# Scores of the fourth attention as three float32r passes over split queries and keys

## The reference

```
k = einsum('ihd,bpd->biph', W_K, x)          # 16 heads of 128, all from 256 inputs
q = einsum('ihd,bpd->biph', W_Q, x)
v = einsum('ihd,bpd->biph', W_V, x)
scores = einsum('biph,biqh->biqp', k, q)     # causal mask, then divided by sqrt(128)
attn = softmax(masked / sqrt(d_head))
z = einsum('biqp,biph->biqh', attn, v)
out = einsum('df,bqf->bqd', W_O, z_flat)
```

## Time and profile before

| | before |
|---|---|
| median of 3 runs (lowest, highest) | 1263.75 us (1261.93, 1264.17) |
| the profiled execution | 1260.36 us |
| its span in the profile | 1258.3 us |
| mean granted clock of PE | 0.986 |
| busy: PE, DVE, ACT, POOL | 93%, 57%, 47%, 14% |

### The profile page before, as it was taken

The page is one execution under the profiler, slowest core; times in us unless marked ns, Lnnn a source line. Parts: engine busy times, 40 slices in busy tenths (PEclk is TensorE's granted clock), DMA queues, the critical chain, the costliest instruction groups (busy, mean ns, idle before and its releaser), DMA issues.

```text
span 1258.3 us, 18298 instructions
## 1 busy us (share of the span) xinstructions
PE 1165.3 (93%) x6204; PEld 773.3 (61%) x6204; DVE 722.7 (57%) x2031; ACT 594.2 (47%) x1498; POOL 175.5 (14%) x225
## 2 busy tenths in 40 slices
PE   5889988898999978999999989989999999999999
PEld 4644444523267554665656558877777777776877
DVE  3778726847144278878797870164444444446573
ACT  2635553677822223554545550255555555555140
POOL 3240023421500400000000010120111121210000
PEclk8979999999999989999999999999999999999999
DMA  8001100140222600000000000220000000000001
GB/s 240 25 8 42 48 30 1 46 141 1 101 70 78 234 0 18 13 13 14 9 9 9 9 1 1 92 96 10 21 22 18 17 26 18 18 9 2 1 1 34
DMA packets 26894, 48.65 MB, mean 39 GB/s; under 512 B 3774, under 2 KB 20126, under 8 KB 25734
## 3 DMA queue, kind: packets, MB, share of 16 engines
q1 hardware_dynamic: 24070, 38.13, 9.5%
q0 software_dynamic: 2736, 9.37, 2.5%
HBM read 40.36 MB, written 9.19 MB: 39 GB/s over the span
## 4 chain that ended last, share of the span: by engine, by line
PE 73%; DVE 13%; ACT 6%; issue 4%; POOL 2%; DMA 1%; SPq 0%; ACTq 0%; DVEq 0%; POOLq 0%
PE bank L1113 9%; PE bank L1104 9%; PE bank L1241 8%; PE bank L1082 5%; PE bank L1108 5%; PE bank L1286 4%; PE bank L1097 4%; PE bank L1236 4%; PE bank L1393 2%; PE bank L1017 2%; PE bank L1006 2%; ACT PT L1638 2%; PE bank L1411 2%; PE bank L927 1%; PE bank L914 1%
## 5 line engine op out<-in xcount | busy, mean ns | idle before, releaser
L1519 ACT COPY R<-bank 128x512 f32<-128x512 f32 (+5 forms) x179 | 96.4, 551 | 258.7 <-PE bank L1113 131.1
L2213 DVE CUSTOM_DVE_ANT_0 bank<-bank,mask_row 128x128 f32<-128x128 f32 (+3 forms) x256 | 126.8, 496 | 149.1 <-PE bank L1104 148.7
L1667 ACT ACTIVATE R<-bank,nm 128x128 f32<-128x128 f32 (+3 forms) x256 | 136.3, 532 | 109.9 <-DVE nm L2213 108.8
L1104 PE MATMUL bank<-R 128*128 128x512 f32 (+3 forms) x384 | 134.3, 434 | 0.0
L1108 PE MATMUL bank<-identf,R 128*128 128x128 f32 x640 | 112.2, 274 | 6.1 <-DVE R L2230 5.5
L1519 ACT COPY PT<-bank 128x128 f32<-128x128 f32 (+3 forms) x256 | 108.6, 425 | 17.0 <-PE bank L1108 16.9
L1108 PEld LDWEIGHTS bank<-identf,R 128*128 128x128 f32 x640 | 79.1, 141 | 40.1 <-DVE R L2230 20.3
L1113 PE MATMUL bank<-PT,R 128*128 128x512 f32 (+3 forms) x256 | 74.7, 435 | 4.2 <-ACT PT L1519 4.2
L1097 PE MATMUL bank<-XNT,W 128*128 128x512 f32 x160 | 77.1, 607 | 0.7 <-ACT XNT L1519 0.7
L1638 ACT ACTIVATE PT<-bank 128x512 f32<-128x512 f32 x128 | 66.5, 608 | 14.1 <-PE bank L1006 14.1
L1082 PE MATMUL bank<-W,R 128*128 128x256 f32 x320 | 69.8, 380 | 2.4 <-ACT R L1519 2.4
(11 more groups left out here) (342 smaller groups left out, 2369.2 us busy)
## 6 DMA issues: line engine op xcount, KB each, us to landing
W<-in_wq SPq DMA_DIRECT2D x32, 128.0 KB, 2.0
W<-in_wo SPq DMA_DIRECT2D x2, 2048.0 KB, 11.2
W<-in_egu SPq DMA_DIRECT2D x1, 2816.0 KB
W<-in_wk SPq DMA_DIRECT2D x20, 128.0 KB, 2.0
R<-xg SPq DMA_DIRECT2D x5, 512.0 KB, 5.0
yg<-R SPq DMA_DIRECT2D x5, 512.0 KB, 3.2
W<-in_wa SPq DMA_DIRECT2D x2, 1024.0 KB, 4.9
W<-in_wb SPq DMA_DIRECT2D x2, 1024.0 KB, 7.4
```

The lines of the kernel that those rows point to most:

```text
L1104: return mm(PS[u % 4][:, 0:n], q[:, t * P:n], k[:, 0:n], start=True, stop=True)
L1519: return nc.scalar.copy(dst, src)
L1667: return fn(Pr[c][:, 0:n], PS[c][:, 0:n], ACT.Exp, scale=-1.0, bias=nm[:, c:c + 1], accum_out=esum[:, c:c + 1])
L2213: return dve.tensor_tensor_reduce(out=s[:, 0:n], in0=s[:, 0:n], in1=mask_row[:, SEQ - n:SEQ], scale=-1.0, scalar=-MASKED, op0=ALU.add, op1 ...
```

## The change

The queries and keys of the fourth attention are kept as high and low halves too, and a score tile becomes three float32r passes, low key * high query first, then high key * low query, then high * high; the first tile of a batch is computed 256 columns wide. ACT empties a projection of q or k by writing the high half (semaphore `high_3`); DVE then subtracts that half from the same bank and writes the low half, and only then is the bank counted as emptied (`pj_used`). The low keys of the two batches lie in `kl3`, one of them in a new tensor. The table `KV3_STEPS` gets another order: q, v, k at steps 0, 1, 2 for batch 0 and at 4, 5, 6 for batch 1, where it was q, k at 1, 3 and v, q, k, v at 4 to 7.

```diff
--- before.py
+++ after.py
@@ -266,6 +266,10 @@
         wap = [x[:, :].rearrange("p (c n) -> p c n", c=DC) for x in (WAH, WAL)]
         wbp = [x[:, :].rearrange("p (m n) -> p m n", m=8) for x in (WBH, WBL)]
         XH3, XL3 = rounded("x3_high", "XNT", 0, [DC, TOK]), rounded("x3_low", "W2", 8192, [DC, TOK])
+        kl3_b1 = sb("kl3_b1", [P, SEQ])
+        qh3, kh3 = rounded("q3_high", "R2", 0, [B, SEQ]), rounded("k3_high", "R2", 1024, [B, SEQ])
+        ql3 = rounded("q3_low", "W2", 6656, [B, SEQ])
+        kl3 = [rounded("k3_low_0", "W2", 7680, [SEQ]), rounded("k3_low_1", "kl3_b1", 0, [SEQ])]
         PAIR = 2 * DH
 
         def split_weight(name, inside, first, n):
@@ -306,6 +310,7 @@
         CORE_A = ("s_ps", "nm", "e_ready", "p_ready", "pt_ps", "pt_sb", "o_ps", "o_used", "pj_ps")
         corea = [{k: sem(f"{k}_{l + 2}") for k in CORE_A + (() if l == 0 else ("pj_used", "w_parts"))} for l in range(2)]
         wq_in, wk_in, wv_in = sem("wq_in"), sem("wk_in"), sem("wv_in")
+        high_3 = sem("high_3")
         xl_ready = sem("xl_ready")
         rope_mul, qk_ready, v_ready = sem("rope_mul"), sem("qk_ready"), sem("v_ready")
         ot_ps, ot_sb, out_ps, s_ready = sem("ot_ps"), sem("ot_sb"), sem("out_ps"), sem("s_ready")
@@ -363,7 +368,7 @@
         TILES = B * TPB
 
 
-        KV3_STEPS = {1: ("q", 0), 3: ("k", 0), 4: ("v", 0), 5: ("q", 1), 6: ("k", 1), 7: ("v", 1)}
+        KV3_STEPS = {0: ("q", 0), 1: ("v", 0), 2: ("k", 0), 4: ("q", 1), 5: ("v", 1), 6: ("k", 1)}
         PJ3 = [(kind, b, 0, half) for b in range(B) for kind, half in (("q", 0), ("k", 0), ("v", 0), ("v", 1))]
         N_FIRST3 = len(PJ3)
         EVENT3 = {}
@@ -1247,7 +1252,12 @@
                     head, b = (n0 + u) // nt, u // TPB % B
                     pe.wait_ge(ca["pj_used"], max(done3("q", b, head), done3("k", b, head)))
                     pe.wait_ge(ca["e_ready"], n0 + u + 1)
-                    score_tile(u, qs[b], ks[b]).then_inc(ca["s_ps"], 1)
+                    t = u % TPB
+                    rows, n = slice(t * P, (t + 1) * P), max((t + 1) * P, 2 * P)
+                    for k, (q, kk) in enumerate(((qh3[:, b, rows], kl3[b][:, 0:n]), (ql3[:, b, rows], kh3[:, b, 0:n]),
+                                                 (qh3[:, b, rows], kh3[:, b, 0:n]))):
+                        ins = mm(PS[u % 4][:, 0:n], q, kk, start=k == 0, stop=k == 2)
+                    ins.then_inc(ca["s_ps"], 1)
 
                 def turn(n0, u):
                     pe.wait_ge(ca["p_ready"], n0 + u + 1)
@@ -1736,14 +1746,15 @@
 
                     kind, b, i, half = PJ3[e]
                     bank = PS[6 + e % 2] if e < N_FIRST3 else PS[7]
-                    if kind != "k":
-                        act.wait_ge(ca["pj_ps"], e + 1)
-                        act.wait_ge(ca["pj_used"], e + 1)
-                        if kind == "v":
-                            copy(vv3[i % 2][b][:, 2 * half:2 * half + 2, :].rearrange("p t e -> p (t e)"), bank[:, :])\
-                                .then_inc(ca["pj_used"], 1)
-                        else:
-                            nc.scalar.mul(qs[b], bank[:, :], DH ** -0.5).then_inc(ca["pj_used"], 1)
+                    act.wait_ge(ca["pj_ps"], e + 1)
+                    act.wait_ge(ca["pj_used"], e + 1)
+                    if kind == "v":
+                        copy(vv3[i % 2][b][:, 2 * half:2 * half + 2, :].rearrange("p t e -> p (t e)"), bank[:, :])\
+                            .then_inc(ca["pj_used"], 1)
+                    elif kind == "k":
+                        copy(kh3[:, b, :], bank[:, :]).then_inc(high_3, 1)
+                    else:
+                        nc.scalar.mul(qh3[:, b, :], bank[:, :], DH ** -0.5).then_inc(high_3, 1)
 
                 def store_output(head, b, unit):
                     act.wait_ge(ca["o_ps"], unit + 1 + 2)
@@ -2275,12 +2286,16 @@
                     p = Pr[c][:, 0:(u % TPB + 1) * P]
                     ts(p, p, erec[:, c:c + 1], None, ALU.mult).then_inc(ca["p_ready"], 1)
 
-                def store_k(e):
+                def store_low(e):
                     kind, b, i, half = PJ3[e]
+                    bank = PS[6 + e % 2 if e < N_FIRST3 else 7]
+                    if kind != "v":
+                        dve.wait_ge(high_3, sum(1 for x in PJ3[:e] if x[0] != "v") + 1)
                     if kind == "k":
-                        dve.wait_ge(ca["pj_ps"], e + 1)
-                        dve.wait_ge(ca["pj_used"], e + 1)
-                        cp(ks[b], PS[6 + e % 2 if e < N_FIRST3 else 7][:, :]).then_inc(ca["pj_used"], 1)
+                        tt(kl3[b][:, :], bank[:, :], plain(kh3[:, b, :]), ALU.subtract).then_inc(ca["pj_used"], 1)
+                    elif kind == "q":
+                        stt(out=ql3[:, b, :], in0=bank[:, :], scalar=DH ** -0.5, in1=plain(qh3[:, b, :]),
+                            op0=ALU.mult, op1=ALU.subtract).then_inc(ca["pj_used"], 1)
 
                 def body(i, last):
                     for v in range(TILES):
@@ -2289,13 +2304,14 @@
                         if v + 4 < nt or not last:
                             maximum(i * nt, v + 4)
                         if (i, v) in EVENT3:
-                            store_k(EVENT3[i, v])
+                            store_low(EVENT3[i, v])
 
                 for b in range(B):
                     if b == 1:
                         ln_scale(3, 1)
                         low_parts((2, 3))
-                    store_k(4 * b + 1)
+                    store_low(4 * b)
+                    store_low(4 * b + 1)
                     if b == 0:
                         for u in range(4):
                             maximum(0, u)
```

## The result

| | before | after |
|---|---|---|
| median of 4 runs, us | 1263.96 (1261.93 to 1265.69) | 1293.70 (1290.84 to 1294.99) |
| ratio, 95% interval | | 1.0233 (1.0215 to 1.0250) |
| profiled execution: span, us | 1258.3 | 1290.9 |

What follows compares the result with a forecast made beforehand. PE's order was taken to bound the kernel; +27.7 us for fourteen heads, +1.7 for the fifteenth pass and +1.4 for the start sum to +30.8, 1294.6 us on the median; range 1280 to 1305.

Steps and rivals of the forecast that it cites:

- The two-link hand-over: Bank 7 behind q: ACT then DVE take 1.71 us against 0.58 of cover; v waits, 2.42 us a head.
- The columns: Fourth attention's score tiles: three passes take 1.935 us for four tiles against 2.16, saving 0.45 us a head.
- The middle price for 384 columns: A float32r pass of 384 columns costs 0.175 us, midway between 0.12 and 0.23; three passes 0.525.
- Values behind k's high half: ACT writes k's high half before the copy the values need; PE waits 0.30 us, 0.60 a head.
- k behind v: One-link hand-over of 0.93 us, partly covered; wait and slow start 0.155 us, 0.31 for two.
- A head: Fourth attention: 18.79 us of columns plus 3.33 of waits make 22.12, +1.98; fourteen heads +27.7.
- The start: First eight projections in two banks: +1.3 and +0.3 for hand-overs, score tiles save 0.2; together +1.4 us.
- the fifteenth pass: Last pass through the projection table, without v: +1.7 us, taken between 0 and +1.98.
- The last head: Head without projections: fewer columns turn into longer waits for the tiles' exponents, change 0.
- The waits before: Old head: 20.14 us less 19.24 of columns leaves 0.90 of waits, which go; chain along PE throughout.
- The clock: Rival 3: waits of 1.1 us lower PE's clock once a head, +25 us, 1320; chance 0.04.

Runs made afterwards that it cites:

- no low halves: Kernel after, but DVE writes low halves of q and k for the first head alone and ACT's high half then frees the bank; 1271.63 us, ratio 1.0080.
- the two kernels without waits: Order q, k, v at steps 1-3 and 5-7, k in bank 6, ACT empties projections before value copies: on kernel after 1246.06 us, on kernel before 1249.46.
- order alone: Kernel before with only the new order of projections, scores still one float32 product; 1263.44 us, ratio 1.0021 to before.
- passes with the old order: Kernel after with the old order of projections (q, k at steps 1, 3; v, q, k, v at 4 to 7); 1317.86 us, ratio 1.0440 to before.
- v in bank 6: Kernel after with v projected into bank 6, the value products' bank, all other work as after; 1256.25 us, ratio 0.9964 to before.

## Why the prediction was right

- **The two-link hand-over**: 1.66 us against 1.71, and some 2.3 us a head against 2.42. Removing the link (no low halves), doubling it, and giving the next projection another bank each moved a head by what the hand-over says. This is shown.
- **The columns**: 0.45 us a head forecast, 0.47 between the two kernels without waits. The middle price for 384 columns holds: 0.53 for three passes.
- **Values behind k's high half, and k behind v**: 0.30 and 0.16, as worked out. Both are read from the rows. The wait before the values is gone in the runs without waits, where v stands between the turned tile and the values, but other edits stand beside it there: that ACT's order alone makes this wait is argued, not shown.
- **A head**: +1.93 us (22.07 less 20.14) against +1.98; 27.0 us in fourteen heads against 27.7.
- **The start and the fifteenth pass**: 3.1 us forecast. In the profiled executions the stage, from the first projection to the last value product, grew by 33.2 us (838.08 to 1170.57 before, 837.58 to 1203.26 after). Less 27.0 for the heads, 6.2 are left; 2.5 of them are a spell at the low clock, below, so that 3.7 remain. The fifteenth pass grew by 1.5 us, where 1.7 was taken as a choice between two bounds, and the start without the spell by 1.3, forecast 1.4. The first head grew by 2.9 instead of 1.93, 1.0 us for which the sum has no term. The last head became 0.1 shorter. First head and fifteenth pass before, then after, in the view of the earlier trace rows:

```profile
856.29:875.97 19.68, 19.57 (x103) 14.59 (x102) 9.38 (x34) 11.02 (x31) 2.25 (x4) 1.00 0.05 15
1137.73:1154.73 17.00, 16.73 (x78) 11.70 (x78) 9.14 (x34) 10.24 (x29) 0.00 (x0) 1.00 0.00 0
```

```profile
859.56:882.14 22.58, 20.26 (x110) 15.62 (x110) 10.29 (x36) 12.84 (x34) 2.26 (x4) 1.00 0.04 13
1169.00:1187.50 18.50, 16.85 (x87) 12.57 (x86) 10.11 (x36) 10.73 (x30) 0.00 (x0) 1.00 0.00 0
```

A part of the first head's excess is in the trace: its q stands at step 0 now and waits until ACT has emptied bank 7 of the start's last v (0.30 us idle ahead of it at 860.31; before, the same q had none). The rest stays open. The hand-over in the start came as forecast: DVE's first piece frees the bank for v 4.1 us after the first projection, where it was 2.86:

```profile
837.58 0.50 PE L1246 MATMUL bank<-x_low,wq_first_high 128*128 128x512 f32 x1 [0.52 <-DVE R L2510]
...
841.68 0.35 PE L1241 MATMUL bank<-wv_first_high,x_low 128*128 128x256 f32 x1 [1.09 <-DVE q_low L2297]
```

- **The waits before**: their sum of 0.90 us a head was right, but the chain did not run along PE through the whole head, as the prediction says of the earlier trace rows, which hold only a part of one. About 0.5 us of the 0.90 lay where v's emptying stood in ACT's stream behind the copy of the value product (the chain is off PE from 896.11 to 897.35). The sum did not suffer, since the new order removes this place as well.
- **The clock**: in the heads it stayed at 1.00 with waits of 1.1 us, so that rival did not come.

The mechanism of the loss is as forecast, link by link. That the whole came within 1 us of the forecast is in part luck: the heads came out 0.7 us below it, and the first head's 1.0 us, which was not foreseen, fills that up.

What I did not see: that the place of the projections could be mended so cheaply. The prediction took bank 7 as given; with a second bank the same change is a gain.

## What to carry to other kernels

When a bank's emptying grows by a second engine, price the hand-over from the last column to the next writer and lay it beside the work that the order puts in between; here that cover decided, with DVE and ACT idle for about half of a head. Before splitting operands for cheaper passes, look for a bank that is idle in just those steps, and for copies in the emptying engine's stream that need not stand in front. The waits that were there before (0.9 us a head) were worth more than the cheaper passes (0.47).

## What the runs showed of the chip

In the profiled execution of the kernel after, PE's clock fell between the first batch's scores and the second batch's projections. Busy time and granted clock of the 5 us up to the first pass of these projections (columns as in the earlier trace rows), and the first twelve passes in the chain, before:

```profile
845.42:850.42 5.00, 2.02 (x11) 0.88 (x9) 3.94 (x10) 2.18 (x6) 1.64 (x2) 1.00 0.41 119
850.42 3.00 PE bank L1241 x12
```

and after, with the 5 us behind as well:

```profile
845.92:850.92 5.00, 2.11 (x12) 1.20 (x11) 4.07 (x12) 2.52 (x8) 0.76 (x1) 0.89 0.25 74
850.92:855.92 5.00, 5.00 (x12) 3.94 (x13) 0.69 (x1) 0.60 (x1) 0.00 (x0) 0.50 0.00 0
850.92 5.46 PE bank L1246 x12
```

At 1.2 GHz a pass of 512 columns takes 0.43 us instead of 0.23, and the twelve take 5.46 instead of 3.00. In all nine profiles PE was busy for 2.02 to 2.12 of the 5 us up to this place and idle for the last 1.45; in four (before, order alone, passes with the old order, v in bank 6) the clock stayed at 2.4 GHz, in the other five it fell to 1.2 for some 3 to 7 us. PE did nearly the same ahead of it in all of them, so the fall is not shown to come from the change, and its 2.5 us stand in one profile after and not in the one before. What decides it stays open.
